# Mask and values turned outside TensorE in a fused audio-tower layer, with the twelfth pair, the expert products and the cosines moved

## The reference, cut to what matters

```python
h = gelu(x[:, 1:] @ W[:256] + x[:, :1] @ W[256:] + b)     # (16, 374, 256)
y = layernorm(h)
h = h + softmax(cosine(y, y)) @ y + y                      # first attention
z = layernorm(h)                                           # the mixture of 8 experts
logits = (z/|z|) @ (s/|s|) - sigmoid(gates)                # (tokens, 8)
mask = logits > 0                  # where no expert is active: the two best
w = softmax over the active experts of relu(logits)
q, k, v = (einsum('tc,ecd,te->td', z, P, mask) for P in (q_proj, k_proj, v_proj))   # d = 128
a = softmax(causal(q @ k.T / sqrt(128))) @ v               # per batch
h = h + einsum('td,edc,te->tc', a, o_proj, mask * w)
```

## Time and profile before

| | us |
|---|---|
| median of 3 runs | 711.19 (710.89 to 711.81) |
| the profiled execution, its own time | 711.77 |
| its span, first to last instruction | 710.1 |
| PE matmuls busy | 705.5 (99%) |
| DVE busy | 579.8 (82%) |
| POOL busy | 400.5 (56%) |
| ACT busy | 378.9 (53%) |

### The profile page before, as it was taken

The page is one execution under the profiler, slowest core; times in us unless marked ns, Lnnn a source line. Parts: engine busy times, 40 slices in busy tenths (PEclk is TensorE's granted clock), DMA queues, the critical chain, the costliest instruction groups (busy, mean ns, idle before and its releaser), DMA issues.

```text
span 710.1 us, 18197 instructions
## 1 busy us (share of the span) xinstructions
PE 705.5 (99%) x5440; PEld 473.1 (67%) x5440; DVE 579.8 (82%) x1455; ACT 378.9 (53%) x808; POOL 400.5 (56%) x655
## 2 busy tenths in 40 slices
PE   9999999999999999999999999999999999999998
PEld 8888666675757666575756666575766657575655
DVE  5788798888879888887979888887988888886736
ACT  4977373554646364563646355464646456364443
POOL 7652325756465566746566575746566674653434
PEclk9999999999999999999999999999999999999999
DMA  9581220202020120202020020202011020201111
GB/s 246 150 188 46 74 45 8 72 3 63 14 63 14 13 65 0 71 7 63 14 55 22 9 68 0 70 8 63 14 23 55 0 71 7 63 17 46 22 68 37
DMA packets 33558, 34.35 MB, mean 48 GB/s; under 512 B 7304, under 2 KB 29304, under 8 KB 33400
## 3 DMA queue, kind: packets, MB, share of 16 engines
q1 hardware_dynamic: 33136, 33.65, 18.4%
q10 hardware_dynamic: 392, 0.32, 0.1%
HBM read 27.70 MB, written 6.26 MB: 48 GB/s over the span
## 4 chain that ended last, share of the span: by engine, by line
PE 98%; issue 1%; POOL 0%; POOLq 0%; DVE 0%; ACT 0%; DVEq 0%
PE bank L1671 76%; PE bank L1734 7%; PE bank L1588 5%; PE bank L1645 3%; PE bank L1577 2%; PE bank L1805 2%; PE bank L1720 1%; PE bank L1783 1%; PE bank L1593 1%; PE bank L1612 1%; PE bank L1756 0%; PE bank L1745 0%; PE bank L1748 0%; POOL region_c L670 0%; POOL region_c L663 0%
## 5 line engine op out<-in xcount | busy, mean ns | idle before, releaser
L1671 PE MATMUL bank<-xm,w_qkv 128*128 128x374 f16 x2304 | 415.7, 322 | 0.0
L1671 PEld LDWEIGHTS bank<-xm,w_qkv 128*128 128x128 f16 x2304 | 220.8, 98 | 139.2
L908 ACT ACTIVATE region_c<-bank,out_w 128x256 f32<-128x256 f32 x180 | 84.8, 471 | 163.2 <-PE bank L1671 162.2
L1274 DVE TENSOR_TENSOR xm<-xT,mask_all 128x1496 f16<-128x1496 f16 x128 | 151.9, 1209 | 0.0
L1671 PE MATMUL bank<-w_o,aoT 128*128 128x512 f16 x540 | 143.3, 379 | 0.0
L1180 DVE SCALAR_TENSOR_TENSOR h<-bank,out_w,h 128x256 f32 (+1 forms) x180 | 86.5, 481 | 48.8 <-ACT region_c L908 43.9
L663 POOL TENSOR_TENSOR region_c<-region_c 128x512 f32<-128x512 f32 x46 | 77.1, 1675 | 27.8 <-ACT region_c L908 22.8
L692 POOL TENSOR_TENSOR exp_hl<-exp,exp_hl 128x128 f16<-128x128 f32 (+2 forms) x48 | 41.9, 875 | 83.7 <-ACT exp_hl L864 83.2
L1671 PEld LDWEIGHTS bank<-w_o,aoT 128*128 128x128 f16 x540 | 50.4, 98 | 39.5
L1159 DVE TENSOR_SCALAR region_b<-h,moments,small 128x256 f32 (+1 forms) x96 | 48.8, 553 | 6.1 <-POOL small L577 6.1
L670 POOL TENSOR_TENSOR region_c<-region_c 128x256 f32<-128x256 f32 x46 | 46.9, 1019 | 8.1 <-POOL region_c L663 7.9
(11 more groups left out here) (200 smaller groups left out, 1067.6 us busy)
## 6 DMA issues: line engine op xcount, KB each, us to landing
mask_all<-d_mask SPq DMA_DIRECT2D x32, 384.0 KB, 3.9
h<-in_x_dram SPq DMA_DIRECT2D x16, 256.0 KB, 5.0
out_dram<-h SPq DMA_DIRECT2D x31, 128.0 KB
rnorm_row<-d_rnorm SPq DMA_DIRECT2D x16, 192.0 KB, 4.1
h<-in_x_dram SPq DMA_DIRECT2D x15, 112.0 KB, 5.4
out_dram<-h SPq DMA_DIRECT2D x15, 112.0 KB
xm<-in_L_ffn_q_proj_dram SPq DMA_DIRECT2D x2, 512.0 KB, 7.5
region_c<-in_L_ffn_k_proj_dram SPq DMA_DIRECT2D x2, 512.0 KB, 6.4
```

The lines of the kernel that those rows point to most:

```text
L908: a.activation(prod[:, prod_buf(n, t), q, :], pair_bank(n, p)[:, C:2 * C], ACT.Copy, scale=weights_out(n)[:, t, 2 * q + 1:2 * q + 2]).then ...
L1274: v.tensor_tensor(xm[:, e, :, 0:T], xT[1][:, :, :, 0:T].rearrange("p a c t -> p (a c) t"), mask_all[:, e, 0:T].unsqueeze(1).broadcast_to([ ...
L1671: last = t_.matmul(dst, left[lp], right[rp], start=(starts and k == 0), stop=(stops and k == 2), skip_group_check=True)
```

## The change

1. **Mask.** `turn_mask` leaves PE, and ACT's copy `turned_mask` goes. The router now writes the 24 columns of the mask (8 experts x 3 tiles) next to each other into a 128x32 tile, DVE turns it in blocks of 32x32 (`turn_mask` on DVE), and SP writes the result in four small DMAs instead of one; the read back over all partitions is the same.
2. **Values.** For batches 0 to 13, `turn_v` leaves PE. Instead ACT copies the values as f32 to SBUF (`values_out`), DVE turns them in 32x32 blocks (`turn_values`, in place of the copy of the low half), SP writes them to memory (`d_v`) and reads them back in four DMAs that put the blocks where they belong, ACT makes the high half (`values_high`) and POOL the low one (`values_low`). Batches 14 and 15 keep `turn_v`.
3. For that, those batches' **v units come before the k units** (`SLOT`), the weights are loaded in that order, and the copies of v and k change places.
4. **Pairs.** Pairs 4 to 10 come one unit later on PE, and the twelfth pair directly behind the eleventh.
5. **Experts ahead of pairs.** On DVE `mask_tokens(f, e)` now stands ahead of the addition of pair 8+e instead of behind it.
6. **Cosines.** The second tile's cosines go ahead of `mask_tokens(m, 5)`, the third tile's ahead of `exp_low(f, 0)`.

```diff
+    rows = d_mask[f, :].rearrange("(r b j) -> b r j", r=SQ, j=SQ)
+    for q in range(P // SQ):
+        sp.dma_start(rows[q][0:NT * E, :], mask_turned[q * SQ:q * SQ + NT * E, :]).then_inc(s_mask_stored, 16)
...
+def values_around(m):                                   # SP
+    sp.wait_ge(s_v_blocks, m + 1).then_inc(s_sp_passed, 1)
+    sp.dma_start(d_v[m, :].rearrange("(p n) -> p n", p=P), v_turned).then_inc(s_v_stored, 16)
+    sp.wait_ge(s_v_stored, 16 * (m + 1)).then_inc(s_sp_passed, 1)
+    if later(m):
+        sp.wait_ge(s_v_tok_ready, 2 * m).then_inc(s_sp_passed, 1)
+    tokens = d_v[m, :].rearrange("(a i t b j) -> b i t a j", a=P // SQ, i=SQ, t=NT, j=SQ)
+    for q in range(P // SQ):
+        sp.dma_start(v_rows[q * SQ:(q + 1) * SQ, :].rearrange("p (t a j) -> p t a j", t=NT, j=SQ),
+                     tokens[q]).then_inc(s_v_loaded, 16)
...
                 if f is not None and not early(m):      # SP's step
                     mask_around(f)
+                if m is not None and by_trip(m):
+                    values_around(m)
...
+def values_low(n):                                      # POOL, behind low_probs(n)
+    pool.wait_ge(s_v_tok_ready, 2 * n + 1).then_inc(s_pool_passed, 1)
+    if later(n):
+        pool.wait_ge(s_pv_done, n).then_inc(s_pool_passed, 1)
+    g.tensor_tensor(v_tok[:, 1, :, :].rearrange("p t d -> p (t d)"), v_rows,
+                    v_tok[:, 0, :, :].rearrange("p t d -> p (t d)"), ALU.subtract).then_inc(s_v_tok_ready, 1)
...
+def values_out(m):                                      # ACT, behind scale_pairs(0, 4)
+    act.wait_ge(s_v_done, m + 1)
+    if later(m):
+        act.wait_ge(s_v_blocks, m)
+    a.activation(v_out[:, 0:T], qkv_bank[2][:, 0:T], ACT.Copy, scale=qkv_out).then_inc(s_v_hi, 1)
+def values_high(n):                                     # ACT, in place of turned_values
+    act.wait_ge(s_v_loaded, 16 * (P // SQ) * (n + 1))
+    if later(n):
+        act.wait_ge(s_pv_done, n)
+    a.activation(v_tok[:, 0, :, :].rearrange("p t d -> p (t d)"), v_rows, ACT.Copy).then_inc(s_v_tok_ready, 1)
...
                     route(f)                            # DVE's step
-                    pairs(2, 4)
+                    pairs(2, 3)
+                    turn_mask(f)
+                    pairs(3, 4)
                     weight_max(f)
-                    head_low(kT, qkv_bank[1], s_k_hi, m + 1, s_k_lo, qkv_out)
+                    if by_trip(m):
+                        turn_values(m)
...
                     for e in range(E - 3):
+                        mask_tokens(f, e)
                         pairs(8 + e, min(9 + e, PAIRS))
-                        mask_tokens(f, e)
...
                     score(n, 2)                         # PE's step
                     pe.wait_ge(s_T1_hi, f + 1)
-                    turn_v(n)
                     M(5)
...
-                    M(15)
-                    turn_mask(f)
+                    M(15, 16)
                     pair(n, 4)
-                    for k in range(7):
-                        M(16 + k)
+                    for k in range(6):
+                        M(17 + k)
                         pair(n, 5 + k)
+                    pair(n, PAIRS - 1)
                     if g1 is not None:
                         turn_first(g1)
                     M(23)
```

More of the change, by code:

```diff
@@ L78, in audio_tower_kernel @@
         xinT = sb("xinT", [P, 2, 2, NC, TP], F16)
+        late = xinT[:, :, :, :, :].rearrange("p a b c t -> p (a b c t)").bitcast(F32)
+        v_out, v_turned, v_rows = (late[:, k * TP:(k + 1) * TP] for k in range(3))
         stats = [sb(f"stats{n}", [P, NT, 6]) for n in (1, 2)]
@@ L368, in prod_buf, with by_trip @@
             return (t + 1) % 2 if final(n) else t % 2
+        SLOT = (0, 2, 1)
+        LAST_TRIP = B - 3
+        def by_trip(b):
+            return not isinstance(b, int) or b <= LAST_TRIP
         def later(b):
@@ L751, in _ @@
             act.wait_ge(s_pad_zeroed, 1)
-            a.activation(unused[:, :], mask16[:, 0, 0:1], ACT.Gelu)
+            a.activation(unused[:, :], zeros16[:, 0:1], ACT.Gelu)
             def split_in(b):
@@ L838, in turned_rows_2 @@
                              ACT.Copy).then_inc(s_T2_hi, 1)
[L840 to L844, removed]
             def route_exp(f):
@@ L1258, in route, with turn_mask @@
                                              ALU.is_lt, ALU.mult))
[L1259 to L1261 removed]
+                v.tensor_tensor(mask16[:, 0:NT * E].rearrange("p (e t) -> p t e", t=NT), lg[:, 0, :, :], M,
+                                ALU.add).then_inc(s_mask_ready, 1)
                 v.tensor_tensor(lg[:, 8, :, :], lg[:, 0, :, :], M, ALU.add).then_inc(s_mask_ready, 1)
                 assert at[0] == RP
+            def turn_mask(b):
+                dve.wait_ge(s_mask_ready, 2 * b + 1)
+                if later(b):
+                    dve.wait_ge(s_mask_stored, 16 * (P // SQ) * b)
+                v.transpose(mask_turned[:, :], mask16[:, :]).then_inc(s_mask_row, 1)
             def mask_tokens(b, e):
@@ L1355, in mask_scores, with turn_values @@
                                        ALU.add, ALU.max, row_max[:, i:i + 1]).then_inc(s_scores_out, 1)
+            def turn_values(m):
+                dve.wait_ge(s_v_hi, m + 1)
+                if later(m):
+                    dve.wait_ge(s_v_stored, 16 * m)
+                v.transpose(v_turned, v_out).then_inc(s_v_blocks, 1)
             def last_values(n):
-                dve.wait_ge(s_v_turned, n + 1)
+                dve.wait_ge(s_v_turned, n - LAST_TRIP)
                 dve.wait_ge(s_pv_done, n)
@@ L1411, in step @@
                     cosines(f, 0)
+                    cosines(f, 1)
                     mask_tokens(m, E - 3)
-                    cosines(f, 1)
+                    cosines(f, 2)
                     exp_low(f, 0)
-                    cosines(f, 2)
                     exp_low(f, 1)
@@ L1677, in unit @@
             def unit(m, which, e):
-                done = (s_q_done, s_k_done, s_v_done)[which]
+                done, slot = (s_q_done, s_k_done, s_v_done)[which], SLOT[which]
                 if which == 0:
@@ L1690, in unit @@
                     if which == 2 and later(m):
-                        pe.wait_ge(s_v_lo, m)
+                        pe.wait_ge(s_v_hi, m)
                 dst = qkv_bank[which][:, 0:T]
                 for c in range(NC):
-                    split_product(dst, [w_qkv[:, p, which, c, e, :] for p in range(2)],
+                    split_product(dst, [w_qkv[:, p, slot, c, e, :] for p in range(2)],
                                   [xm[:, e, p * NC + c, 0:T] for p in range(2)],
                                   e == 0 and c == 0, e == E - 1 and c == NC - 1,
-                                  done if (e == E - 1 or which == 2) and c == NC - 1 else None)
+                                  done if (e == E - 1 or which == 1 or which == 2 and not by_trip(m)) and c == NC - 1 else None)
             def dots(f, t):
@@ L1750, in logits @@
                 last.then_inc(s_logits_done, 1)
-            def turn_mask(f):
-                pe.wait_ge(s_mask_ready, 2 * (f + 1))
-                pe.wait_ge(s_T2_lo, f + 1)
-                for t in range(NT):
-                    last = t_.transpose(as16(turn[1] if later(f) else turn[0], TP)[:, t * P:(t + 1) * P], mask16[:, t, :], ident16[:, :])
-                last.then_inc(s_mask_turned, 1)
             def score(n, i):
@@ L1863, in M @@
                         for u in us:
-                            unit(m, u // E, u % E)
+                            unit(m, SLOT[u // E] if by_trip(m) else u // E, u % E)
                 def N(fn, *a):
```

101 lines of the change are left out of this document (61 added, 40 removed).

## The result

The changed kernel takes **724.97 us** (median of 5 runs, 724.62 to 725.58), the one before 711.81 in the same job (710.89 to 712.2). The ratio is 1.0189, 95% interval 1.0176 to 1.0201: the change costs 13.2 us where I forecast a gain of 6.5. The profiled execution took 724.97, its span 723.2.

The account below looks back on a forecast made before the run. PE's summed instructions were taken to bound the kernel, with no wait in a step. Removed transposes, 7.18 us, less 0.7 for waits at pair 11 gave 6.5 us: 704.7 us forecast, 703.6 to 705.5 (0.6), wider range 703.4 to 708.5.

Parts of the forecast that it names:

- What leaves PE: On PE, the removed transposes of values (4.62 us) and mask (2.56 us) together save 7.18 us.
- The values' way: Values through DVE, memory and back: DVE's transpose 0.55 to 1.35 us, landing 3 to 7 us before ACT needs them.
- The mask's way: Mask through DVE and SP's four writes: landed at 373.0, needed by expert 0's product on DVE at 373.08.
- just fits: The mask's landing at 373.0 against the need at 373.08; later by x, PE would wait x at pair 11.
- Pair 11: PE's wait for DVE's addition of pair 9: 0.3 us spare if DVE is free, 0.7 us lost over 14 steps.
- mostly one short and one that varies: DVE's two expert products ahead of pair 9's addition, each 1.02 to 1.53 us: the mix assumed for PE's wait.
- a smaller gain: Rival: two long products or a dear transpose make PE wait at pair 11, 705.5 to 709.6 us; chance 0.2.
- slower: Rival: mask 2 us late gives 732 us, or values' read at 20 us gives 788 us; chance 0.12.
- The charge: Allowance for PE's wait at pair 11: 0.05 us a step, 0.7 us over 14 steps.
- Cosines: Second tile's cosines earlier on DVE: no gain by itself, but keeps DVE in time with PE 0.49 us faster.
- My bounds of 8.6 and 11.3 us: Estimates for the values' read of 1536 pieces of 128 bytes, taken from the two nearest rows.
- the rival's 78 us: The skill's 19 times slower strided copy applied to a 4.1 us load, under the late-values rival; chance 0.12 with late mask.

Follow-up runs that it names:

- run 8: The changed kernel with part 5 undone and k's low half moved on DVE behind the next step's first cosines: 705.00 us.
- Run 9: The changed kernel, orders kept, with DVE turning the mask ahead of pair 2's addition and SP reading the norms back behind the mask: 710.6 us.
- Run 6: The changed kernel, but POOL waits for the second expert product before its subtraction: 713.21 us.
- run 2: The changed kernel with part 4 alone undone, DVE's products still ahead of the pairs' additions: 715.53 us.
- run 3: The changed kernel with parts 4 and 5 both undone: 708.65 us.
- run 5: The changed kernel with two of the mask's four writes issued from ACT's queue: 724.63 us.
- run 1: The changed kernel with part 5 undone, so the additions go ahead of the products again: 707.75 us.
- run 7: The changed kernel with parts 5 and 6 undone, so the cosines go back behind the products as well: 715.69 us.
- Run 4: The kernel before the change with parts 4 and 5 alone, mask and values still turned by PE: 715.15 us.

## Why the prediction was wrong

**What leaves PE: right.** 0.49 us a step was worked out, and run 8 shows a step of 40.00 against 40.50. Its whole gain in the same job is 711.56 - 705.00 = 6.6 us of the 7.18; where the other 0.6 us are was not looked into. The pairs stood where they were put: by the prediction's clock, which is 5.99 us behind this trace's (pair 3 at 364.03 - 0.33 there, at 369.69 here), pair 4 at 366.25 (372.24) and pair 9 at 374.24 (380.22).

**The values' way: right.** DVE's transpose of them takes 0.58 us, near the low bound of 0.55, the mask's 0.20. The reads were issued from 381.30 on and had landed at 385.9, on the prediction's clock 379.9, where 383 to 387 was worked out and 389.83 needed. ACT never waits for them. POOL's low half took 0.91 us and fell into the gap as intended: POOL still waits 2.00 us for the moments behind it.

**The mask's way: the step that failed first, by half a microsecond.** On the prediction's clock the writes began at 365.76 (365.7 worked out), the last went at 367.28 (367.1), the reads at 369.36 (369.1), and the mask landed at 373.53 (373.0). Each of the four terms added 0.06 to 0.27, all in one direction; the need was at 373.08. The prediction called this "just fits". With no spare, an error of half a microsecond in a sum of four terms decides, and I gave that case 0.12. DVE stood idle for the mask for 0.57 us.

**Pair 11: the step that failed in size.** It priced a mask that is late by x at x, and a product at 1.02 to 1.53 by two rows, "mostly one short and one that varies". Both are wrong in the same way. A product's length is not scatter: it depends on which engine starts first. In the earlier trace rows the first product ends 0.79 us behind an operation of POOL that was about to end (its subtraction ran to 374.36), and so does the second, behind one in full course (its addition, to 376.28). POOL's two rows of the kernel before:

```profile
372.75 1.61 POOL L624 TENSOR_TENSOR xhl<-region_b,xhl 128x768 f16<-128x768 f32 x1
374.31 1.97 POOL L663 TENSOR_TENSOR region_c<-region_c 128x512 f32<-128x512 f32 x1
```

The prediction's reason against long products, that the short one exists beside POOL's work too, misread this. When the mask is late by 0.57, the product no longer starts ahead of POOL's subtraction but 0.53 behind its start, and takes 1.88 instead of about 0.95. So 0.66 late at its start (379.64, where pair 7's addition would have let it go at 378.98) became 1.6 late at its end, and the second product met POOL's addition and took 1.60. The rival "a smaller gain" had two long products (a wait of 0.6 us), the rival "slower" a late mask; neither had that one brings the other. The charge was 0.05 us a step, measured are 1.42 at pairs 10 and 11. Run 9 takes the delay away and leaves the orders: 0.20, still four times the charge. Run 6 takes POOL's head start away and leaves half of the delay, 0.29: no wait at the pairs. So at the pairs either alone costs little, and the two together cost 1.42 us a step. Forecast and result lie 19.7 us apart (6.5 faster, 13.2 slower). In 13 steps the 1.37 us above the charge are 17.8, and the 0.19 of the next paragraph are 2.5: 20.3. The 0.6 between the two lie outside these steps and are not split up.

**Not foreseen: 0.19 us a step at the second norm's rows.** It is in runs 2, 3, 5, 6 and 9 too. DVE runs two products there (rows of the changed kernel, then of run 8):

```profile
353.31 2.26 DVE L1340 TENSOR_TENSOR xm<-xT,mask_all 128x1496 f16<-128x1496 f16 x2
```

```profile
344.46 1.80 DVE L1340 TENSOR_TENSOR xm<-xT,mask_all 128x1496 f16<-128x1496 f16 x2
```

They are 0.46 longer in the one. In the changed kernel POOL starts its low half of the exponentials, at 353.83 for 0.95 us, ahead of the second product, which then ends at 355.57, 0.79 behind it; in run 8 POOL comes at 345.41, 1.0 us behind the start of the two, when the second is already under way. The norm's chain stands behind these products. The runs go with it: the two products take 2.25 or 2.26 us in runs 2, 3, 5, 6 and 9, which have the wait, and 1.80 to 1.84 in runs 1, 7 and 8, which have not. Run 4 has 2.26 without a wait, but its PE still has the transposes and is later by them. That this is the cause is read from the rows; no run changed it alone.

**Cosines: right in its second half, without a size.** The prediction said that they give nothing by themselves, but keep DVE in time when PE is 0.49 us faster. The second is so: in the kernel with the faster PE, leaving the cosines where they were costs 0.67 a step (run 7 against run 1, 7.9 us), more than the transposes are worth. The first, the cosines alone on the kernel before, no run tested.

**The orders.** Parts 4 and 5 cost 0.2 a step even with the mask in time (runs 4 and 9). With the mask's new way, neither of them takes 708.65 us (run 3), part 4 alone 707.75 (run 1), part 5 alone 715.53 (run 2), both 724.97. So part 5 is what turns the kernel's gain into a loss, and part 4 makes it larger: the addition for which PE waits next was put behind a product whose own input was late.

## What to carry to other kernels

Where a prediction finds that something "just fits", work out what happens if it misses by half a microsecond: what starts instead, and what does that hold up? Put an instruction with an uncertain DMA in front of it behind, not ahead of, the one for which the bottleneck engine waits. When an operation shows two durations in a trace, look at what the other engine had running at its start before calling it scatter.

## What the runs showed of the hardware

- **An expert product on VectorE and a two-input operation on GpSimd take turns, whole instructions at a time.** The product (two inputs in SBUF) takes 0.92 to 0.95 us when POOL has nothing running; that holds for all 405 such products in the eleven traces. If one of POOL's wide two-input operations runs already, the product ends about 0.8 us behind that operation's end, whatever time it started (2.14, 1.88, 1.60 and 1.53 us are such cases). Of the 1003 products that start beside an operation of POOL, 949 end 0.79 to 0.81 behind the end of it; the other 54 take no more than 0.94, beside operations of three columns, or ones that were about to end, or ones that began within 0.02 us of the product. If the product starts first, by 0.13 us in runs 4 and 9, POOL's subtraction takes 2.30 and 2.31 instead of 1.61. Not every operation of VectorE is held up: the addition of a pair, which reads one of its inputs from PSUM, takes 0.47 us beside POOL's 1.97 (at 381.44). The Trainium skill, "SBUF — State Buffer", section "SBUF: two separate sides", says that the shared port pair is an exclusive lock that the first to start holds for its whole instruction. The traces agree for these operations, and I should have used that rule to read the two rows.
- **VectorE's transposes in blocks** take 0.58 us for 128x384 in f32 and 0.20 us for 128x32 in f16, where PE's path cost 0.33 and 0.16 of PE's time.
- **Small pieces through memory** were no trouble: the write of 192 KB by rows lands in 4.3 us, and each of the four reads of 48 KB in pieces of 128 bytes in 2.3 us (medians of the page of the changed kernel). All four together, from the first issue to the last landing, took 4.6 us (381.30 to 385.9). My bounds of 8.6 and 11.3 us for the read were about twice too long, and the rival's 78 us did not show.
